# Channel attention on one NeuronCore: other taps for the key extremes, their chains, the projections and the weighted sums

## What is computed

```
q = einsum('bchw,oc->bohw', x, w_q)
kmap, vmap = the same projections of the padded x with w_k, w_v
kwin = concatenate([kwin[:, :half] + rel_h, kwin[:, half:] + rel_w])
attn = softmax(q[..., None] * kwin, axis=-1)      # over the 49 places, per channel
out = sum(attn * vwin, axis=-1)
```

## Time and profile before

| what | before |
|---|---|
| median of 3 runs | 7996.73 us (7989.87 to 7998.88) |
| the profiled execution, its own time | 7993.27 us |
| its span in the profile | 7991.6 us |
| channel attention: first and last `shift` | 3315.0 and 7303.1 us |
| busy over the whole span | PE 94%, DVE 71%, POOL 57%, ACT 46% |
| granted TensorE clock in the four tiles used below | 1.00 |

### The profile page before, as it was taken

One profiled execution on the slowest core, in us unless ns is written; L12 is line 12 of the kernel. 1 busy time (PEld: TensorE's weight loads), 2 busy tenths in 40 slices (PEclk: granted clock), 3 DMA queues, 4 the chain that ended last, 5 costly groups with the idle time before them and its releaser, 6 DMA issues. The chain is left out here.

```text
span 7991.6 us, 141890 instructions
## 1 busy us (share of the span) xinstructions
PE 7529.3 (94%) x55106; PEld 6489.6 (81%) x55106; DVE 5666.6 (71%) x8853; ACT 3670.7 (46%) x7040; POOL 4566.2 (57%) x2002
## 2 busy tenths in 40 slices
PE   5999998989998999599999999999999999997999
PEld 4777776879997776388888888888888888886999
DVE  5666665334443555688888888888888888896664
ACT  3655655423332332255555555555555555554222
POOL 3555552023332000388888888888888788886232
PEclk9999998999999999799999999999999999998999
DMA  3111113865557873100000000000000000002452
GB/s 142 61 58 67 60 58 122 282 161 144 144 147 194 234 210 109 29 20 23 27 18 17 20 23 27 18 18 19 24 27 18 17 20 24 27 9 93 138 164 78
DMA packets 633018, 617.21 MB, mean 77 GB/s; under 512 B 465525, under 2 KB 498421, under 8 KB 627174
## 3 DMA queue, kind: packets, MB, share of 16 engines
q1 hardware_dynamic: 581318, 483.44, 21.8%
q0 software_dynamic: 33856, 96.69, 3.3%
q10 hardware_dynamic: 17376, 30.54, 1.0%
HBM read 397.01 MB, written 193.76 MB: 74 GB/s over the span
## 5 line engine op out<-in xcount | busy, mean ns | idle before, releaser
L1909 POOL TENSOR_TENSOR e_ev<-e_se,e_v 128x2048 f32<-128x2048 f32 (+1 forms) x896 | 3307.7, 3712 | 760.6 <-ACT e_se L1847 758.1
L1847 ACT ACTIVATE e_se<-e_stage 128x512 f32<-128x512 f32 x3136 | 1867.8, 597 | 1851.4 <-PE e_stage L1679 1792.9
L1998 DVE SCALAR_TENSOR_TENSOR e_stage<-e_k,e_rl,e_qp 128x512 f32<-128x512 f32 x3136 | 2290.5, 747 | 340.7 <-ACT e_se L1847 285.7
L1686 PE MATMUL e_pe_sum<-e_ident,e_se 128*128 128x128 f32 x12544 | 1880.6, 272 | 16.5 <-ACT e_se L1847 12.3
L1686 PE MATMUL e_pv_sum<-e_ident,e_ev 128*128 128x128 f32 x12544 | 1875.4, 273 | 0.5 <-POOL e_ev L1909 0.5
L1686 PEld LDWEIGHTS e_pe_sum<-e_ident,e_se 128*128 128x128 f32 x12544 | 1550.6, 140 | 259.1 <-ACT e_es L1835 21.8
L1686 PEld LDWEIGHTS e_pv_sum<-e_ident,e_ev 128*128 128x128 f32 x12544 | 1477.2, 140 | 204.6 <-issue 203.2
L1679 PE MATMUL e_stage<-e_top,e_minus 128*128 128x512 f32 x3136 | 1507.8, 481 | 89.2 <-DVE e_stage L1998 85.6
L911 POOL DMA_DIRECT2D agg<-c_ot x384 | 334.6, 874 | 878.7 <-ACT c_ot L989 769.1
L403 POOL TENSOR_TENSOR a_pr<-a_pr,a_rden 128x480 f32<-128x480 f32 x512 | 494.1, 985 | 547.6 <-DVE a_rden L636 547.6
L1679 PEld LDWEIGHTS e_stage<-e_top,e_minus 128*128 128x128 f32 x3136 | 595.5, 190 | 143.6 <-DVE e_stage L1998 99.7
(11 more groups left out here) (175 smaller groups left out, 11567.5 us busy)
## 6 DMA issues: line engine op xcount, KB each, us to landing
qkv<-b_ot SPq DMA_DIRECT2D x120, 512.0 KB, 5.9
c_xt<-qkv SPq DMA_DIRECT2D x384, 160.0 KB, 3.8
agg<-c_ot POOLq DMA_DIRECT2D x384, 160.0 KB, 2.5
f_ws<-in_L_w_sets SPq DMA_DIRECT2D x32, 1152.0 KB, 7.9
a_xb<-in_x SPq DMA_DIRECT2D x24, 768.0 KB, 5.1
a_xr<-in_x SPq DMA_DIRECT2D x32, 512.0 KB, 3.8
x<-a_xr SPq DMA_DIRECT2D x32, 512.0 KB, 2.7
b_xc<-x SPq DMA_DIRECT2D x32, 512.0 KB, 5.8
```

What stands on the lines that cost most here:

```text
L1686: last = nc.tensor.matmul(acc[:, c * PART:(c + 1) * PART], lhsT=src[:, c * PART:(c + 1) * PART], rhs=ident[:], is_transpose=True, start=j ...
L1847: nc.scalar.activation(se[(t * K2 + o) % NSE][:, i], stage[:, bank_of(t, j), :], ACT.Exp)\
L1909: nc.gpsimd.tensor_tensor(split(ev[(t * NG2 + g) % NEV][:, 0:size]), split(se[(t * K2 + o) % NSE][:, i:i + size]), window(v[h], h, u, o, i ...
L1998: nc.vector.scalar_tensor_tensor(rows(stage[:, bank_of(t, j), :]), win, rl[:, h, o:o + 1], rows(qp[:]), ALU.add, ALU.mult).then_inc(multip ...
```

## The change

No instruction is added or taken away but for the places of the tables. The pair steps and reductions go to other taps (three of them at tap 11, two at tap 12; the minima behind the maxima, up to tap 39). The links of the chain get a table of their own, which starts at tap 23 of u = 0, puts up to two links at one tap, and ends at entry 103, that is tap 5 of the next half's first tile. The two openings for maxima now wait only for the maxima. The projections move by up to three taps, and the weighted sums no longer follow at twelve taps but at the taps of `V_AT` (at some taps none, at others two). Division, turning back, addition and statistics move by one to three taps.

```diff
-        PROJ_AT = ({0: "K0", 7: "K1", 14: "K2", 24: "Q1", 29: "Q2"}, {2: "V0", 6: "V1", 12: "V2"})
+        PROJ_AT = ({11: 'K2', 22: 'Q1', 5: 'K1', 32: 'Q2', 1: 'K0'}, {8: 'V1', 13: 'V2', 2: 'V0'})
-        E_LAG, V_LAG = 2, 12
+        E_LAG = 2
+        V_AT = [13, 14, 14, 15, 16, 16, 18, 19, 19, 21, 22, 23, 24, 25, 25, 26, 26,
...
-        INVERT_AT = (3, 5, 7, 9)
+        INVERT_AT = (4, 7, 8, 9)
-        DIVIDE_AT, BACK_AT, ADD_AT = 12, 20, 23
-        STATS_AT = (25, 27)
+        DIVIDE_AT, BACK_AT, ADD_AT = 13, 17, 22
+        STATS_AT = (24, 25)
-        KEYS_AT, VALUES_AT, NEAR_AT = 1, 18, 3
+        KEYS_AT, VALUES_AT, NEAR_AT, PAIRS_AT = 1, 17, 3, 20
...
+        NEAR = [(11, 'K1', 0, 0), (11, 'K1', 1, 0), (11, 'K1', 0, 1), (12, 'K1', 0, 2), (12, 'K1', 0, 3),
...
+        EXT_AT = [23, 27, 29, 32, 34, 34, 40, 43, 45, 49, 52, 52, 55, 57, 58, 62, 62,
+                  66, 66, 69, 71, 74, 77, 77, 80, 78, 82, 84, 87, 90, 91, 99, 102, 103]
...
             def open_extreme(H, s):
-                act.wait_ge(near_step, nears(H + 1))
+                if OPENS.index(s) < 2:
+                    act.wait_ge(near_step, nears(H) + near_before(H, 1 + max(i for i, x in enumerate(near_of(H)) if x[2] == 0)))
+                else:
+                    act.wait_ge(near_step, nears(H + 1))
...
-                if j == NEAR_AT and H % 2 == 1 and H + 1 + u < NH2:
-                    (carry_near, carry_pairs)[u](H + 1 + u)
+                if (u, j) == (0, NEAR_AT) and H % 2 == 1 and H + 1 < NH2:
+                    carry_near(H + 1)
+                if (u, j) == (1, PAIRS_AT) and H % 2 == 1 and H + 2 < NH2:
+                    carry_pairs(H + 2)
```

More of the change, by code:

```diff
@@ L1465, in channel_attention @@
         FRESH, WAS = HALO, R2
-        PROJ_AT = ({0: "K0", 7: "K1", 14: "K2", 24: "Q1", 29: "Q2"}, {2: "V0", 6: "V1", 12: "V2"})
+        PROJ_AT = ({11: 'K2', 22: 'Q1', 5: 'K1', 32: 'Q2', 1: 'K0'}, {8: 'V1', 13: 'V2', 2: 'V0'})
         ROWS_OF = {"0": (PAD, PAD), "1": (FRESH, RT), "2": (FRESH + RT, RT)}
-        E_LAG, V_LAG = 2, 12
+        E_LAG = 2
+        V_AT = [13, 14, 14, 15, 16, 16, 18, 19, 19, 21, 22, 23, 24, 25, 25, 26, 26,
+                28, 30, 31, 31, 32, 32, 34, 36, 37, 38, 39, 39, 41, 43, 44, 46, 46,
+                47, 49, 50, 51, 51, 52, 53, 54, 55, 57, 58, 58, 59, 60, 61]
         Q_AT = NTAP - NST
-        INVERT_AT = (3, 5, 7, 9)
+        INVERT_AT = (4, 7, 8, 9)
         NINV = len(INVERT_AT)
-        DIVIDE_AT, BACK_AT, ADD_AT = 12, 20, 23
-        STATS_AT = (25, 27)
+        DIVIDE_AT, BACK_AT, ADD_AT = 13, 17, 22
+        STATS_AT = (24, 25)
+        BACK_TAKES = [max((j, p) for j, p in PROJ_AT[u].items() if j < BACK_AT)[1] for u in range(2)]
+        FREED = [min([(j, p) for j, p in PROJ_AT[u].items() if j > BACK_AT], default=(0, None))[1] for u in range(2)]
         NORM_AT = 30
-        KEYS_AT, VALUES_AT, NEAR_AT = 1, 18, 3
+        KEYS_AT, VALUES_AT, NEAR_AT, PAIRS_AT = 1, 17, 3, 20
         PIECES = ((0, 3), (3, 3), (6, 2))
[L1477 to L1480, removed]
+        NEAR_FIRST = [(6, 'K0', 0, 0), (6, 'K0', 1, 0), (7, 'K0', 0, 1), (8, 'K0', 1, 1)]
+        NEAR = [(11, 'K1', 0, 0), (11, 'K1', 1, 0), (11, 'K1', 0, 1), (12, 'K1', 0, 2), (12, 'K1', 0, 3),
+                (15, 'K2', 0, 0), (16, 'K2', 1, 0), (18, 'K2', 0, 1), (20, 'K2', 0, 2), (23, 'K2', 0, 3),
+                (26, 'K1', 1, 1), (30, 'K1', 1, 2), (31, 'K1', 1, 3), (34, 'K2', 1, 1), (38, 'K2', 1, 2),
+                (39, 'K2', 1, 3)]
         CHAIN = (K2 + 1, K2 + 2)
@@ L1483, in channel_attention @@
         TOP_AT = [2 * CHAIN[0] + (w + 1) * CHAIN[1] for w in range(2)]
-        EXT_FREE = [(0, j) for j in range(34, NTAP)] \
-            + [(1, j) for j in range(NTAP - 2) if j not in (*INVERT_AT, DIVIDE_AT, ADD_AT)]
         OPENS = [0, CHAIN[0], 2 * CHAIN[0], 2 * CHAIN[0] + CHAIN[1]]
-        LINK_AT = [sum(3 if i - 1 in OPENS else 1 for i in range(1, s + 1)) for s in range(NEXT_ + 1)]
-        EXT_AT = [EXT_FREE[LINK_AT[s] * len(EXT_FREE) // LINK_AT[-1]] for s in range(NEXT_)]
+        EXT_AT = [23, 27, 29, 32, 34, 34, 40, 43, 45, 49, 52, 52, 55, 57, 58, 62, 62,
+                  66, 66, 69, 71, 74, 77, 77, 80, 78, 82, 84, 87, 90, 91, 99, 102, 103]
         block = ctx.enter_context(nc.Block())
@@ L1724, in step @@
                 h, u = tile_of(t)
-                late = j == V_LAG
-                if not late and (t * NTAP + j >= V_LAG or not first):
-                    sum_weighted(n, *before(t, j, V_LAG), first=first)
+                due = [(t - 1, i) for i in range(NTAP) if V_AT[i] == NTAP + j and (t or not first)] \
+                    + [(t, i) for i in range(NTAP) if V_AT[i] == j]
+                for t0, i in due[:1]:
+                    if i:
+                        sum_weighted(n, t0, i, first=first)
                 shift(n, t, j)
@@ L1730, in step @@
                     sum_exponential(n, *before(t, j, E_LAG), first=first)
-                if late:
-                    sum_weighted(n, t, 0, first=first)
+                for t0, i in due:
+                    if not i or (t0, i) != due[0]:
+                        sum_weighted(n, t0, i, first=first)
                 H = n * HALVES + t // 2 + 1
@@ L1739, in step @@
                             free = n * TPB + t - 1
-                        elif p == "Q1" and n * TPB + t:
+                        elif p == FREED[u] and n * TPB + t:
                             free = n * TPB + t
@@ L1744, in step @@
                     whole = H < NH2
-                    back(n, t - 1, made(H, ("K2", "V2")[u]) if whole else 0, nears(H, "K2") if whole and u == 0 else 0)
+                    back(n, t - 1, made(H, BACK_TAKES[u]) if whole else 0, nears(H, BACK_TAKES[u]) if whole and BACK_TAKES[u][0] == "K" else 0)
             for i in range(NST):
@@ L1754, in _ @@
             all_bands(step)
[L1755 to L1758, removed]
+            for j in range(NTAP - E_LAG, NTAP):
+                sum_exponential(NB - 1, TPB - 1, j)
+            for j in range(NTAP):
+                if V_AT[j] >= NTAP:
+                    sum_weighted(NB - 1, TPB - 1, j)
             back(NB - 1, TPB - 1)
@@ L1876, in step @@
                     normalise(n + 1)
[L1877 to L1880, removed]
+                for s in OPENS:
+                    if EXT_AT[s] == u * NTAP + j + 2 * NTAP and H > 1:
+                        open_extreme(H - 1, s)
+                    if EXT_AT[s] == u * NTAP + j and H < NH2:
+                        open_extreme(H, s)
                 if j == Q_AT and not (final and t == TPB - 1):
@@ L2044, in step @@
                 H = n * HALVES + t // 2 + 1
+                at = t % 2 * NTAP + j
+                for s in range(NEXT_):
+                    if EXT_AT[s] == at + 2 * NTAP and H > 1:
+                        extreme_step(H - 1, s)
                 if H < NH2:
                     for s, step_ in enumerate(near_of(H)):
-                        if t % 2 == 0 and step_[0] == j:
+                        if step_[0] == at:
                             near_step_of(H, s)
                     for s in range(NEXT_):
-                        if EXT_AT[s] == (t % 2, j):
+                        if EXT_AT[s] == at:
                             extreme_step(H, s)
```

## The result

The change runs in 7951.58 us in the median of 6 runs (7945.34 to 7965.22), the kernel before in 7992.29 (6 runs, 7983.27 to 7998.88). The ratio is 0.9952, with a 95% interval of 0.9939 to 0.9964: faster by about 0.5%. Forecast were 7940 us and a range of 7912 to 7966. The sign and the place were right, the gain was forecast at 56 us and is 41 between the medians.

What follows compares the result with a forecast made beforehand. PE was taken as the bound, its idle time mostly due to VectorE. Gains of 3.6 us per band, 57 over 16 bands, plus 4 at new images, less about 5, gave 56: 7940 us, range 7912 to 7966.

Steps and rivals of the forecast that it cites:

- The place and the bound: PE is busy nearly all the time; some 6.8 us per band of its idle time comes from VectorE.
- Third tile, second tile: Per band, third tile gains 1.1 us; second loses 0.5 to 0.6, its last opening waiting for VectorE's `top`.
- The first tile: First tile of a band (odd half): PE stalls 2.6 us instead of 5.4, so 2.8 us gained.
- Tap 11: Taps 11 and 12, first tile: VectorE 6.3 us against PE's 1.99 + 1.55, lead 1.8, short by 1.0 us.
- the fourth tile: Fourth tile of each band: 0.3 us gained.
- New images: First tiles at three new images: 67.0 us instead of 71.8, 4 us in all beyond ordinary bands' gain.
- the ledger: Tap-by-tap sum of VectorE's lead against PE's steps, over all tiles for both orders; trusted to about 0.5 us a band.
- the 61 us that the terms gave: Gain summed as 57 us over 16 bands plus 4 us at new images.
- the forecast case: Gain of 35 to 80 us, chance 0.66.
- The lump of 5 us: Whole kernel: about 5 us taken off the gain for what the ledger can't see, partly small waits that stay.
- The rule on the bubbles: Repeating PE gaps can mean too few buffers; no bank is added, so the time would stay at 7997 us.
- The rival by the Trainium skill: More gain, chance 0.08: PE's products have hidden slack; loads' busy share leaves 36 us per band; 7888 us at 109 gained.

Runs made afterwards that it cites:

- The version above: All tables chosen anew by the mended ledger, same work, against the kernel before: 7837.59 us against 7989.26, ratio 0.9817; also called the last version.

## Why the prediction was right, and where it fell short

- **The place and the bound** were right: PE sets the time, its idle time comes from VectorE's lead, and the order of one engine has to be read against the steps of the other. The version above confirms the price of PE's work to 0.4 us in 240.
- **Third tile, second tile** came out as worked out (1.1 gained, 0.5 lost). The mechanism of the second, an opening that waits for `top` ahead of the normalisation, shows in the waits.
- **The first tile** was the step that failed in size: "Tap 11 [...] with a lead of 1.8. Short by 1.0". Measured is a lead of 1.3 and a loss of 1.8 (0.26 us at tap 11, 1.58 at tap 12). The missing lead is the wait of ScalarE's carry; the run with the chain's end two taps earlier brings the lead to 1.86 and gives 0.5 us of the tile back. The other part is 0.33 us of VectorE in the crowded taps, read from the timeline above; no run takes it apart alone, but with the lead mended the loss is 1.35, so it is what is left over the 1.0. With 0.2 us in the fourth tile the band gained 1.1 us less than forecast, 17 us in sixteen bands. The first band's first tile gained only 0.3 us, 1.5 less than the others.
- **New images**: they were to gain 4 us more than ordinary bands, and gained about 3 less. Their first tile takes 68.6 and 68.4 us and not 67.0: PE waits 2.6 us at K1's projection, where the ledger had 2.1, and then stands at tap 12 as in other bands (1.59 and 1.36 us). The third one took 69.9, by a fall of the clock that no term of the sum has. The tile that prepares the even half of a new image rose from 63.4 to 63.8 where its like in other bands fell by 1.1. The trace shows K0's steps at taps 6 to 8 taking the lead away there: it is 0.06 us at tap 9 and 0.64 at tap 11 (done at 4196.23, shift at 4196.87), against 1.86 in an ordinary third tile, and PE stands 0.55 and 0.69 us at taps 11 and 12. No run moves K0's steps alone. Of the 61 us that the terms gave before the deduction of 5, the ordinary bands thus take 17, the new images 7 and the first band about 1.5; that leaves 35.5, near the measured 34.8.
- **Luck.** The median is 7951.58 and the forecast 7940, but 5 us of the 41 lie behind the stage and 1.4 are one fall of the clock less. The stage's own 34.8 us are just at the lower edge of the forecast case (35 to 80). The lump of 5 us deducted for what the ledger cannot see covered a fifth of the 26 us by which the terms were too high.
- **A ledger that is 0.3 us off per tile before the change** was good evidence for its form but not for places that only the change uses: full-size extras in a row and a chain that ends in the next band occur nowhere in the kernel before.
- **The rule on the bubbles** (the Trainium skill, "Perfetto Trace Analysis", Optimization Strategy) did not hold here: it says that such gaps can mean too few buffers, and the same three banks are enough for tiles without idle PE time. The rival by the Trainium skill ("Perfetto Trace Analysis", Identifying the Most-Contended Engine), 36 us of headroom per band by the loads' busy share, did not come either: in the last version, where PE is busy all the time, the loads are busy 213 of 240 us. Half a projection keeps PE for 0.88 us with only two loads of 0.19 us each.

## What to carry to other kernels

When a static order feeds one saturated engine, keep two running sums, the work of the feeding engine and that of the fed one, and look at their difference at every step; a wait removed ahead of a ceiling is worth little (0.6 us of a tile for a wait of 1.93), and one table changed alone can cost more than the whole change brings (+77 us). The bound engine's own steps are a tool too: moving its work so that a long step stands where the feeder has an extra costs no work and was worth 23 to 33 us here. Price what the new order does for the first time (extras in a row, waits across a tile's edge) as unknown, however well the sum fits the old order.

## What was unexpected of the hardware

A VectorE operation took about 0.1 us more when the next one waited for it than with a multiplication in between: two pair steps, with a reduction behind them that waits too, 1.43 us start to start instead of 1.20 to 1.22, and two reductions 2.47 instead of 2.37. What in the engine costs this was not tried.

In the ordinary bands' windows the granted clock was 1.00, with PE busy from 91% to 100%, so filling the last gaps cost no clock. At new images it fell to 0.50 behind waits of PE, but not behind each: of two waits of 2.6 us in the same trace one was followed by a fall and one was not.
